# Attention masks as TensorE products, paired weight pieces, an earlier first expert tile and eight row buffers in an attention and mixture-of-experts kernel

## The chip, the cores and the metric

One core of one Trainium2 chip runs the kernel. The metric is the device time of one execution in microseconds (us). The core has TensorE (PE, matrix products and transposes), VectorE (DVE), ScalarE (ACT), GpSimd (POOL), the SyncE queue (SP), which here only issues transfers, and 16 DMA engines.

## What is computed

Sixteen batches of 100 queries attend to 1,444 keys of width 128. A mixture of eight experts (top two) follows over all 1,600 tokens. Cut to what matters:

```python
def xattn(input, memory, mask, w_input, dot_scale):   # input (16,100,128), memory (16,1444,128)
    att = (input @ w_input.T) + (input * dot_scale) @ memory.T - 1e+30 * mask[:, None, :]
    return softmax(att) @ memory

def moe(x, W_router, W_gate, W_up, W_down):           # 8 experts, F = 512
    gates, indices = top_k(softmax(x @ W_router.T), 2); gates = gates / gates.sum(-1)
    for e in experts:
        out += weight_e * ((silu(x @ W_gate[e].T) * (x @ W_up[e].T)) @ W_down[e].T)
    return out

x = x + tanh(g_xattn) * xattn(layernorm(x), ctx_1024, mask, ...)
x = x + tanh(g_ffn) * moe(layernorm(x), ...)
```

## The kernel before

Every engine has its own program, written out by hand in order; semaphores connect them. There is no scheduler, so what stands ahead of an instruction in its engine's program is what it queues behind.

**Attention, 16 steps.** Step b on TensorE is: the scores of batch b (L970, three products of 512, 512 and 420 columns, in float32 two passes each), the transposes of the softmax weights of batch b-1 (L980, 12), the transposes of the keys of batch b+1 (L957, 12), then the products of the softmax weights of b-1 with the keys (L990, 12, two passes), with the transpose of the second layer norm's result of batch b-2 (L998), its router product (L1004) and, every other step, the ranks (L1015, L1017) between them. ACT moves two thirds of the transposed keys out of PSUM and applies the score's scale and bias (L583), moves the transposed weights (L593) and computes the exponential (L627). DVE moves the last third (L702), adds the mask and takes the row maximum in one instruction (L741), and does residual, statistics, top two and ranks. POOL does the layer norms, the gates and scatters of the token rows into a DRAM table `slots`, sorted by expert (L508).

**Transfers of the attention.** All are issued by SP in program order: keys (720 KB a batch), a mask row broadcast to 100 partitions (564 KB a batch), and a 256 KB piece of the gate and up weights in each step. The masks of batches 0 and 1 come raw and ACT scales them (`scale_mask`); for the others DVE scales all 16 rows once (L869), ACT stores them to DRAM (L645) and SP broadcasts from there. ACT rounds each weight piece (L604, `round_weights`) after the exponential of a step, and DVE takes the rounding's rest (L729, `split_weights`). The 2 MB of down weights go out in four parts in steps 10 to 13, between the others (L338).

**Expert tiles.** There are 32 tiles of 128 token rows. The first eight (`EARLY`) are taken from what the first ten batches are known to fill, so that they can start before routing ends. In tile step k TensorE transposes the rows of tile k+1 (L1061), does gate and up of tile k (L1071 to L1073, six products of 512 columns), transposes the hidden values of tile k-1 (L1082) and multiplies tile k-2 by the down weights (L1093). ACT rounds the transposed rows (L653), applies silu (L662) and empties the hidden and result banks (L668, L674); DVE takes the rest of the rounding (L878) and multiplies gate, up and routing weight (L901). POOL scatters the results (L556). SP loads the rows into four buffers (L385), each load after the hidden values of four tiles before. Ahead of tile 8's load SP waits for `late_ready`, for the scatters of the last batches, and for eight clears of table tails (`clear_tail`, L388 reads a row number into a register, L389 issues the transfer); these stand behind the load of row block 6 and ahead of that of block 7.

**End.** When all results are stored, SP loads the first result of each token in four parts and ACT the second one (L408, L684), DVE adds both to x (L914, L917), and SP stores each part when its second addition is done (L411).

## Time and profile before

| | us |
|---|---|
| three runs, median | 287.19 |
| lowest and highest | 286.39, 293.68 |
| the profiled execution, its own time | 289.13 |
| its span in the trace | 287.3 |

Mean granted TensorE clock over the span: 0.941. By the page's own sums TensorE is busy 84% of the span (and its weight loads 69%), DVE 48%, ACT 47%, POOL 44%. Such shares are means over stages with different limits, so the reading below goes stage by stage.

### The profile page before, as it was taken

What the parts mean: (1) busy time and instruction counts of PE and PEld (TensorE: products, weight loads), DVE (VectorE), ACT (ScalarE), POOL (GpSimd) and SP (SyncE); (2) the same over time, 40 slices, a digit from 0 to 9 for tenths busy, and PEclk for the clock granted to TensorE, in tenths of its full rate; (3) what the DMA queues carried; (4) which work ended last, traced back from release to release, by engine and by line L of the source; (5) the groups of instructions that cost most, each with busy time, mean ns of one, the idle gap of its engine ahead of it and who ended that gap; (6) DMA issues with size and microseconds to landing.
All of it is one profiled execution on the core that took longest, in us unless ns stands there. A gap on an engine that the chain in (4) does not pass through costs nothing.

```text
span 287.3 us, 5727 instructions
## 1 busy us (share of the span) xinstructions
PE 241.9 (84%) x1602; PEld 199.2 (69%) x1603; DVE 137.4 (48%) x437; ACT 136.1 (47%) x295; POOL 126.0 (44%) x227
## 2 busy tenths in 40 slices
PE   7888498999999999999698896099999999999300
PEld 6657387777778887777578685089888878888200
DVE  1246238766666666675575553314343333433033
ACT  1466257555556665554546542226454554545100
POOL 4070403334754678877836877203323323233300
PEclk9999989999999999999899999669999999999855
DMA  5968877887788789999711022211111111110055
GB/s 135 219 191 202 191 191 205 204 195 205 196 201 204 199 207 220 224 230 244 241 44 50 5 65 75 65 28 49 38 56 40 55 37 37 55 37 30 27 182 161
DMA packets 19175, 37.65 MB, mean 131 GB/s; under 512 B 3722, under 2 KB 11090, under 8 KB 19150
## 3 DMA queue, kind: packets, MB, share of 16 engines
q1 hardware_dynamic: 15398, 32.65, 45.6%
q0 software_dynamic: 2560, 3.77, 4.5%
q10 hardware_dynamic: 1192, 0.92, 1.1%
q8 instruction: 13, 0.21, 0.3%
q14 instruction: 12, 0.10, 0.1%
HBM read 32.05 MB, written 5.27 MB: 130 GB/s over the span
## 4 chain that ended last, share of the span: by engine, by line
PE 60%; DMA 20%; SPq 5%; issue 5%; ACT 3%; DVE 2%; POOL 2%; another core or an unknown queue 1%; POOLq 0%; DVEq 0%; ACTq 0%
PE psum L990 12%; DMA ctx_sb<-in_ctx 11%; PE psum L1093 8%; PE psum L970 8%; PE psum L1071 6%; PE psum L957 6%; PE psum L1073 5%; DMA x_all<-in_x 5%; PE psum L1072 5%; PE psum L1082 5%; DMA ctx_sb<-results 3%; PE psum L980 2%; SPq L388 2%; PE psum L1061 1%; ACT probsT L593 1%
## 5 line engine op out<-in xcount | busy, mean ns | idle before, releaser
L556 POOL DMA_INDIRECT results<-y_sb,dest x32 | 30.8, 963 | 64.2 <-DVE dest L890 51.9
L990 PE MATMUL psum<-ctx_sb,probsT 120*100 120x128 f32 (+1 forms) x384 | 48.5, 278 | 1.0 <-issue 1.0
L901 DVE SCALAR_TENSOR_TENSOR scores<-probs,row_in,psum 128x512 f32<-128x512 f32 x32 | 23.9, 747 | 47.3 <-ACT probs L662 45.4
L990 PEld LDWEIGHTS psum<-ctx_sb,probsT 120*100 120x100 f32 (+1 forms) x384 | 44.4, 171 | 1.2 <-issue 1.2
L970 PE MATMUL psum<-ctxT,qT 128*100 128x512 f32 (+1 forms) x96 | 42.6, 581 | 0.2 <-issue 0.2
L662 ACT ACTIVATE probs<-psum 128x512 f32<-128x512 f32 x32 | 19.1, 597 | 43.4 <-PE psum L1073 36.2
L508 POOL DMA_INDIRECT slots<-pair_rows,slot_i x32 | 33.0, 1032 | 8.8 <-issue 8.8
L957 PE MATMUL psum<-identity,ctx_sb 120*128 120x120 f32 (+1 forms) x192 | 26.0, 291 | 11.7 <-DMA ctx_sb<-in_ctx 4.7
L1093 PE MATMUL psum<-w_down,hidT 128*128 x256 | 34.9, 280 | 0.8 <-ACT y_sb L674 0.6
L1093 PEld LDWEIGHTS psum<-w_down,hidT 128*128 128x128 f32 x256 | 32.0, 196 | 1.2 <-issue 1.2
L957 PEld LDWEIGHTS psum<-identity,ctx_sb 120*128 120x128 f32 (+1 forms) x192 | 22.3, 154 | 14.8 <-DMA ctx_sb<-in_ctx 7.7
L1071 PE MATMUL psum<-w_hi,rowT_hi 128*128 x64 | 28.8, 449 | 2.1 <-issue 1.7
L741 DVE CUSTOM_DVE_ANT_0 scores<-psum,maskb 100x1444 f32<-100x1444 f32 x16 | 26.5, 1659 | 7.6 <-PE psum L970 7.6
L437 POOL TENSOR_SCALAR var<-mv 100x1 f32<-100x1 f32 x16 | 4.8, 299 | 54.3 <-DVE mv L724 53.9
L970 PEld LDWEIGHTS psum<-ctxT,qT 128*100 128x100 f32 x96 | 15.4, 171 | 18.0 <-issue 18.0
L1073 PE MATMUL psum<-w_hi,rowT_lo 128*128 x64 | 25.7, 402 | 0.0
L583 ACT ACTIVATE ctxT<-psum,wi_col,ds_col 128x484 f32<-128x484 f32 (+1 forms) x32 | 22.6, 749 | 6.5 <-PE psum L957 3.8
L1072 PE MATMUL psum<-w_lo,rowT_hi 128*128 x64 | 25.5, 398 | 0.0
L627 ACT ACTIVATE probs<-scores,negmax 100x1444 f32<-100x1444 f32 x16 | 24.0, 1497 | 0.0
L588 ACT ACTIVATE qT<-psum 128x100 f32<-128x100 f32 x16 | 4.0, 250 | 39.8 <-PE psum L980 37.0
L593 ACT ACTIVATE probsT<-psum 120x400 f32<-120x400 f32 (+1 forms) x48 | 20.8, 510 | 3.6 <-PE psum L980 3.6
L702 DVE TENSOR_SCALAR ctxT<-psum,ds_col,wi_col 128x480 f32<-128x480 f32 x16 | 12.4, 776 | 19.4 <-PE psum L957 19.4
(126 smaller groups left out, 377.3 us busy)
## 6 DMA issues: line engine op xcount, KB each, us to landing
ctx_sb<-in_ctx SPq DMA_DIRECT2D x16, 720.0 KB
maskb<-mask_scaled SPq DMA_DIRECT2D x14, 564.1 KB
w_raw<-in_w_experts SPq DMA_DIRECT2D x16, 256.0 KB, 9.7
row_in<-slots SPq DMA_DIRECT2D x32, 65.0 KB
w_down<-in_w_experts SPq DMA_DIRECT2D x4, 512.0 KB
maskb<-in_mask SPq DMA_DIRECT2D x2, 564.1 KB
ctx_sb<-results SPq DMA_DIRECT2D x4, 200.0 KB
ctx_sb<-results ACTq DMA_DIRECT2D x4, 200.0 KB
```

Of the source, the lines that this page charges most:

```text
L508: nc.gpsimd.indirect_dma_start(slots, bass.IndirectOffsetOnAxis(ap=slot_i[:, b, j:j + 1], axis=0), pair_rows[:, b, j, :], None).then_inc(s ...
L556: nc.gpsimd.indirect_dma_start(results, bass.IndirectOffsetOnAxis(ap=dest[:, s:s + 1], axis=0), y_sb[:, s, :], None).then_inc(y_stored[s], 16)
L627: nc.scalar.activation(probs[0:Q, :], scores[0:Q, :], ACT.Exp, bias=negmax[:, b % 2:b % 2 + 1], accum_out=rowsum[:, b % RING:b % RING + 1] ...
L741: nc.vector.tensor_tensor_reduce(out=scores[0:Q, :], in0=scores_ps[0:Q, 0:K], in1=maskb[:, b % 2, :], scale=1.0, scalar=LOWEST, op0=ALU.ad ...
L901: nc.vector.scalar_tensor_tensor(out=hidden[k % 2], in0=silu[k % 2], scalar=row_in[:, s, D:D + 1], in1=up_ps[k % 2], op0=ALU.mult, op1=ALU ...
L957: last = nc.tensor.transpose(ring_ps[g][:, at:at + rows[c]], ctx_sb[0:rows[c], s, c, :], identity[0:rows[c], 0:rows[c]])
L970: last = nc.tensor.matmul(scores_ps[0:Q, n:n + m], qT[:, b % 2, :], ctxT[:, n:n + m], start=True, stop=True)
L990: last = nc.tensor.matmul(attn_ps[0:Q, 0:D], probsT[0:rows[c], c, :], ctx_sb[0:rows[c], b % RING, c, :], start=(c == 0), stop=(c == CHUNKS ...
L1071: nc.tensor.matmul(ps, rowT_hi[:, o, :], hi, start=True, stop=False)
L1072: nc.tensor.matmul(ps, rowT_hi[:, o, :], lo, start=False, stop=False)
L1073: last = nc.tensor.matmul(ps, rowT_lo[:, o, :], hi, start=False, stop=True)
L1093: last = nc.tensor.matmul(y_ps, hidT[:, o, c * P:(c + 1) * P], w_down[:, bass.ds(e * F + c * P, P)], start=(c == 0), stop=(c == FC - 1))
```

## The change

1. The masks of batches 0 and 1 are no longer loaded as broadcasts. The 16 raw mask rows go out second on SP's queue; `select` is a matrix whose row b is one for batch b; a product `select[:, b]` with the scaled mask rows starts the accumulation in the scores' bank and the score products add to it. DVE's addition gets a zero row for these two. The store of the scaled rows moves ahead of ACT's evictions. TensorE's three warming products behind the first transposes are gone.
2. Weight pieces follow a table `ROUNDED`: none before step 2, two in steps 6, 8 and 10, the last in step 14. The down weights go out all behind the loop. x comes in four parts.
3. Tile 0: its rows are transposed into a bank of the scores, and its gate and up products stand ahead of the last batch's attention products.
4. There are eight row buffers; SP issues all eight early row blocks and then five tail clears; ACT issues the other three, one after each of its tile steps 4, 5 and 6. The tables of the late tiles come one tile step earlier on DVE.
5. At the end SP loads parts 0 and 2 of both results, ACT parts 1 and 3; the output is laid out by query, so that each query's four batches are one run in DRAM (the host puts it back in place).

The core of the diff:

```diff
+MASKED = 2
+ROUNDED = {2: (0,), 3: (1,), 4: (2,), 5: (3,), 6: (4, 5), 7: (6,), 8: (7, 8), 9: (9,), 10: (10, 11), 11: (12,),
+           12: (13,), 13: (14,), 14: (15,)}
+SP_TAILS = 5
...
-        row_in = sb("row_in", [P, RING, ROW])
+        row_in = sb("row_in", [P, YRING, ROW])
...
             load_x(0)
+            sp.dma_start(mask_rows, mask).then_inc(mask_raw, 16)
             load_ctx(0)
-            load_raw_mask(0)
             load_x(1)
-            sp.dma_start(mask_rows, mask).then_inc(mask_raw, 16)
             load_ctx(1)
-            load_raw_mask(1)
             load_x(2)
             load_ctx(2)
-
-            for b in range(B - 2):
+            sp.wait_ge(mask_stored, 16)
+            load_mask(MASKED)
+            load_ctx(RING - 1)
+            load_x(3)
+
+            for b in range(1, B - 2):
                 sp.wait_ge(scores_done, b + 1)
-                if b == 0:
-                    sp.wait_ge(mask_stored, 16)
                 load_mask(b + 2)
-                if b == 0:
-                    load_ctx(RING - 1)
-                load_weights(b)
-                if 1 <= b and b + RING - 1 < B:
+                for c in ROUNDED.get(b + 1, ()):
+                    load_weights(c)
+                if b + RING - 1 < B:
                     sp.wait_ge(attn_raw, b)
                     load_ctx(b + RING - 1)
...
-                if b >= 10:
-                    load_down(b - 10)
-            load_weights(B - 2)
-            load_weights(B - 1)
+            for m in range(4):
+                load_down(m)
...
-                wait(sp, hidden_done, n - RING + 1)
+                wait(sp, hidden_done, n - YRING + 1)
...
-                if n == EARLY - 2:
+                if n == EARLY - 1:
                     sp.wait_ge(tails_ready, 1)
-                    for e in range(E):
+                    for e in range(SP_TAILS):
                         clear_tail(e)
...
-            for m in range(CUTS):
+            for m in range(0, CUTS, 2):
                 sp.dma_start(first_sb[:, m * CUT:(m + 1) * CUT, :], pairs(0, m)).then_inc(first_loaded[m], 16)
+            for m in range(0, CUTS, 2):
+                sp.dma_start(second_sb[:, m * CUT:(m + 1) * CUT, :], pairs(1, m)).then_inc(second_loaded[m], 16)
             for m in range(CUTS):
                 sp.wait_ge(second_added, m + 1)
-                sp.dma_start(out[m * CUT:(m + 1) * CUT, :, :].rearrange("b q d -> q b d"),
-                             x_all[:, m * CUT:(m + 1) * CUT, :]).then_inc(out_stored, 16)
+                sp.dma_start(out[:, m * CUT:(m + 1) * CUT, :], x_all[:, m * CUT:(m + 1) * CUT, :]).then_inc(out_stored, 16)
...
-                    if b == 0:
-                        scale_mask(1)
-                    if b >= 1:
-                        round_weights(b - 1)
-                    if b == B - 1:
-                        round_weights(B - 1)
+                    for c in ROUNDED.get(b, ()):
+                        round_weights(c)
...
             copy_qT(0)
+            act.wait_ge(mask_scaled_done, 1)
+            act.dma_start(mask_scaled, mask_rows).then_inc(mask_stored, 16)
             evict_ctxT(0, 0)
             evict_ctxT(0, 1)
-            scale_mask(0)
...
+            def between(n):
+                e = SP_TAILS + n - 4
+                if 0 <= n - 4 and e < E:
+                    if e == SP_TAILS:
+                        act.wait_ge(tails_ready, 1)
+                    clear_tail(e)
+
+            rowT_high(0, 0, first_rowT_ps)
             nc.scalar.activation(warm[:, :], wi_col[:, :], ACT.Silu)
-            copy_xn2T(B - 2)
-            over_tiles(act, tile_step)
+            for g in range(GROUPS):
+                copy_probsT(B - 1, g)
+            over_tiles(act, tile_step, between)
...
+            nc.vector.memset(maskb[:, 1, :], 0.0)
+            dve.wait_ge(identity_done, 1)
+            nc.vector.tensor_copy(select[:, :, :], identity[0:B, 0:MASKED].unsqueeze(2).to_broadcast([B, MASKED, Q])).then_inc(select_done, 1)
             statistics1(0)
             statistics1(1)
+            dve.wait_ge(mask_raw, 16)
+            nc.vector.tensor_scalar(mask_rows, mask_rows, NEG, None, ALU.mult).then_inc(mask_scaled_done, 1)
...
+            def add_mask(b):
+                pe.wait_ge(select_done, 1)
+                pe.wait_ge(mask_scaled_done, 1)
+                wait(pe, scores_done, b)
+                for n in range(0, K, 512):
+                    m = min(512, K - n)
+                    nc.tensor.matmul(scores_ps[0:Q, n:n + m], select[:, b, :], mask_rows[:, n:n + m], start=True, stop=False)
+
             def score(b):
+                if b < MASKED:
+                    add_mask(b)
...
             transpose_ctx(0)
-            keep_warm(3)
...
+            pe.wait_ge(scores_done, B)
+            transpose_rows(0, 0, first_rowT_ps)
             transpose_probs(B - 1, False)
+            pe.wait_ge(early_ready, 1)
+            pe.wait_ge(w_lo_done, B)
+            gate_up(0, 0)
             ranks(LAST - 1)
             attend(B - 1, 0, 2)
-            pe.wait_ge(early_ready, 1)
             pe.wait_ge(probsT_done, B * GROUPS)
-            transpose_rows(0, 0)
+            transpose_rows(0, 1)
             attend(B - 1, 2, GROUPS)
-            transpose_xn2(B - 2)
-            pe.wait_ge(w_lo_done, B)
-            pe.wait_ge(down_loaded, 16 * 4)
```

On TensorE, from the transposes of the first keys (into `psum` from `ctx_sb`) to the second scores (from `ctxT` and `qT`), the program stood so before:

```order
L957 MATMUL psum<-identity,ctx_sb 128x120 x8
L935 MATMUL psum<-identity 128x128 x3
L970 MATMUL psum<-ctxT,qT 100x512 x2
L970 MATMUL psum<-ctxT,qT 100x420
L939 MATMUL psum<-identity,xn 128x100
L957 MATMUL psum<-identity,ctx_sb 128x121 x4
L957 MATMUL psum<-identity,ctx_sb 128x120 x8
L935 MATMUL psum<-identity 128x128 x4
L970 MATMUL psum<-ctxT,qT 100x512 x2
```

And it stands so now, with the mask rows in the first columns of `w_down`:

```order
L973 MATMUL psum<-identity,ctx_sb 128x120 x8
L983 MATMUL psum<-w_down,select 100x512 x2
L983 MATMUL psum<-w_down,select 100x420
L996 MATMUL psum<-ctxT,qT 100x512 x2
L996 MATMUL psum<-ctxT,qT 100x420
L955 MATMUL psum<-identity,xn 128x100
L973 MATMUL psum<-identity,ctx_sb 128x121 x4
L973 MATMUL psum<-identity,ctx_sb 128x120 x8
L951 MATMUL psum<-identity 128x128 x4
L983 MATMUL psum<-w_down,select 100x512 x2
L983 MATMUL psum<-w_down,select 100x420
L996 MATMUL psum<-ctxT,qT 100x512 x2
```

A mask product of the same shape as the score's now stands ahead of each of the first two scores, and the three warming products (L935) are gone.

On TensorE at the hand-over to the tiles, from the transposes of the last softmax weights to tile 0's gate and up (reads of `row_in` are row transposes, of `pair_rows` the layer norm's), before:

```order
L980 MATMUL psum<-identity,probs 120x100 x8
L1015 MATMUL psum<-chosen,before 100x24
L1017 MATMUL psum<-passed,ones 100x24
L990 MATMUL psum<-ctx_sb,probsT 100x128 x8
L1061 MATMUL psum<-identity,row_in 128x128
L990 MATMUL psum<-ctx_sb,probsT 100x128 x4
L998 MATMUL psum<-identity,pair_rows 128x100
L1061 MATMUL psum<-identity,row_in 128x128
L1066 TENSOR_LOAD tile_expert
L1066 ISA x2
L1071 ISA
L1071 MATMUL psum<-w_hi,rowT_hi 128x512
```

and now (the first products of gate and up, and what is behind the six):

```order
L1087 MATMUL psum<-identity,row_in 128x128
L1007 MATMUL psum<-identity,probs 121x100 x4
L1007 MATMUL psum<-identity,probs 120x100 x8
L1092 TENSOR_LOAD tile_expert
...
L1099 MATMUL psum<-w_hi,rowT_lo 128x512
L1042 MATMUL psum<-chosen,before 100x24
L1044 MATMUL psum<-passed,ones 100x24
L1017 MATMUL psum<-ctx_sb,probsT 100x128 x8
L1087 MATMUL psum<-identity,row_in 128x128
L1017 MATMUL psum<-ctx_sb,probsT 100x128 x4
L1025 MATMUL psum<-identity,pair_rows 128x100
L1087 MATMUL psum<-identity,row_in 128x128
```

Tile 0's row transpose and its six products moved from behind the last attention products (L990, now L1017) to ahead of them; tile 1's row transpose took the place between them.

ACT's queue had no tail clears before. Now, behind the result copy (L674) of its tile step 4, and in the same way of steps 5 and 6:

```order
L646 ACTIVATE rowT_hi<-psum 128x128
L659 ACTIVATE probs<-psum 128x512
L666 ACTIVATE hidT<-psum 128x512
L674 ACTIVATE y_sb<-psum 128x128
L649 TENSOR_LOAD tail_row
L649 ISA x2
L650 ISA
L650 DMA slots<-empty 128x130
```

Three of SP's eight clears went to ACT, each tied to the end of one of its tile steps.

## Rows read from the trace of the kernel before

**Rows 1.** The page: DMA share in tenths, GB/s, in 40 slices of 7.2 us.
```profile
DMA  5968877887788789999711022211111111110055
GB/s 135 219 191 202 191 191 205 204 195 205 196 201 204 199 207 220 224 230 244 241 44 50 5 65 75 65 28 49 38 56 40 55 37 37 55 37 30 27 182 161
```
**Rows 2.** Windows: stretch, length, busy of PE, PEld, DVE, ACT, POOL, clock, DMA share, GB/s.
```profile
50.24:125.06 74.82, 73.44 (x543) 58.43 (x542) 49.03 (x163) 44.34 (x89) 44.55 (x78) 1.00 0.86 207
177.11:185.89 8.78, 0.00 (x0) 0.00 (x1) 2.68 (x8) 1.25 (x3) 3.88 (x4) 0.77 0.24 69
185.89:192.03 6.14, 5.73 (x19) 4.76 (x20) 1.11 (x3) 1.47 (x3) 0.00 (x0) 0.50 0.09 22
192.03:269.23 77.20, 75.93 (x496) 65.75 (x494) 27.31 (x74) 39.38 (x102) 25.52 (x27) 1.00 0.15 42
```
**Rows 3.** Timeline of the start: start, length, engine, line, what, idle before.
```profile
8.42 2.64 PE L957 MATMUL psum<-identity,ctx_sb 121*128 121x121 f32 x12 [1.67 <-ACT qT L588]
...
12.14 3.79 PE L970 MATMUL psum<-ctxT,qT 128*100 128x512 f32 x6
...
16.75 1.46 PE L957 MATMUL psum<-identity,ctx_sb 121*128 121x121 f32 x12 [0.73 <-DMA ctx_sb<-in_ctx]
...
19.27 2.64 PE L970 MATMUL psum<-ctxT,qT 128*100 128x512 f32 x6 [0.17 <-issue]
```
**Rows 4.** Timeline of the start, steps 1 to 3.
```profile
27.79 2.59 PE L970 MATMUL psum<-ctxT,qT 128*100 128x512 f32 x6
...
34.13 0.63 ACT L604 ACTIVATE w_hi<-w_raw 128x512 fp32r<-128x512 f32 x1 [6.71 <-DMA w_raw<-in_w_experts]
...
35.45 2.64 PE L957 MATMUL psum<-identity,ctx_sb 121*128 121x121 f32 x12 [3.87 <-ACT probsT L593]
```
**Rows 5.** The chain that ended last: start, length, what. Scores of steps 4 and 6.
```profile
50.24 2.42 PE psum L970 x6
...
66.82 2.42 PE psum L970 x6
```
**Rows 6.** Timeline of TensorE at steps 13 to 15.
```profile
125.06 2.59 PE L970 MATMUL psum<-ctxT,qT 128*100 128x512 f32 x6
...
133.58 2.59 PE L970 MATMUL psum<-ctxT,qT 128*100 128x512 f32 x6
...
140.15 2.09 PE L957 MATMUL psum<-identity,ctx_sb 121*128 121x121 f32 x12 [2.79 <-DMA ctx_sb<-in_ctx]
...
146.30 2.59 PE L970 MATMUL psum<-ctxT,qT 128*100 128x512 f32 x6
```
**Rows 7.** Timeline of the hand-over: tile 0's products on TensorE, ranks, SP's tail clears.
```profile
160.20 0.49 PE L1071 MATMUL psum<-w_hi,rowT_hi 128*128 x1 [0.68 <-issue]
...
168.99 0.28 PE L1015 MATMUL psum<-chosen,before 100*100 100x24 f32 x2
...
170.84 12.49 SPq L389 DMA_DIRECT2D slots<-empty  x8
```
**Rows 8.** Timeline of TensorE, the head of tile step 6.
```profile
185.89 0.47 PE L1061 MATMUL psum<-identity,row_in 128*128 128x128 f32 x1 [8.78 <-DMA row_in<-slots]
```
**Rows 9.** The chain: an SP register step, a clear, row block 7; timeline: block 8.
```profile
180.46 0.70 SPq L388
...
183.01 0.33 SPq L389
...
184.10 1.74 DMA row_in<-slots
...
186.17 0.36 SPq L385 DMA_DIRECT2D row_in<-slots  x1
```
**Rows 10.** Timeline of the end: first, second and last additions.
```profile
277.08 0.69 DVE L914 TENSOR_TENSOR x_all<-x_all,ctx_sb 100x512 f32<-100x512 f32 x1 [11.63 <-DMA ctx_sb<-results]
277.88 0.69 DVE L917 TENSOR_TENSOR x_all<-x_all,ctx_sb 100x512 f32<-100x512 f32 x1
...
282.05 0.69 DVE L914 TENSOR_TENSOR x_all<-x_all,ctx_sb 100x512 f32<-100x512 f32 x1 [0.17 <-DMA ctx_sb<-results]
283.22 0.69 DVE L917 TENSOR_TENSOR x_all<-x_all,ctx_sb 100x512 f32<-100x512 f32 x1 [0.47 <-DVE x_all L914]
```

135 lines of the change are left out of this document (71 added, 64 removed).

## The prediction, made before the changed kernel ran

> **What bounds the kernel now.** I read the chain of work that ended last, then the timeline stretch by stretch, then windows of the same stretches. Five stages came out.
>
> *Start, 0 to 50.24.* The first scores run from 12.14, the second from 19.27, the third from 27.79, the fifth from 50.24 [rows 3, 4, 5]. An undisturbed pair of steps takes 66.82 - 50.24 = 16.58 us [rows 5], but the third to fifth took 22.45. ACT had waited 6.71 us for the first weight piece, with the softmax weights of batch 1 queued behind, and TensorE 3.87 us for ACT [rows 4].
>
> *Attention, 50.24 to 125.06.* TensorE is busy 73.44 of 74.82 us, at a DMA share of 0.86 and 207 GB/s [rows 2]. TensorE is the bound and transfers are near theirs.
>
> *Its end.* Steps 13 and 14 took 146.30 - 125.06 = 21.24 us, with a 2.79 us wait for the last keys [rows 6]. In these slices the DMA digits stand at 9 and the rate at 230 to 244 GB/s, the highest of the trace [rows 1]: the down weights share the queue with these keys.
>
> *Tiles.* Tile 0's products begin at 160.20 [rows 7]. Step 5 ends at 177.11, then TensorE does nothing for 8.78 us [rows 2, 8]: block 7 stands behind eight clears on SP, 170.84 to 183.33 [rows 7]. The next step runs at clock 0.50 and takes 6.14 us; after it 27 steps take 77.20 us, 2.86 each [rows 2].
>
> *End.* DVE's last addition ends at 283.9, the span at 287.3 [rows 10].
>
> **The change, part by part.** *Masks.* Added are two groups of six passes of the scores' shape: 2.59 us each at full clock [rows 4]. The first group begins right behind the key transposes, at 8.42 + 2.64 = 11.1 [rows 3], where warming products stood. The first scores took 3.79 us, which is about three passes at half clock and three at full [rows 3], so the clock rose near 14.6; from 11.1 the group takes 4.3 us, to 15.4, and the scores end at 18.0. It can begin there only if DVE has scaled the 16 rows. DVE's zero row and `select` come before; nothing in the trace shows a fill of 1,444 columns, I bound it between nothing and the 1.66 us of DVE's mask instruction of that width and take that it is hidden: DVE is idle until x lands. The keys of batch 1 came at 16.75 [rows 3]; 1.13 MB of raw masks less in the queue, at some 200 GB/s [rows 1], bring them before 18. Transposes and warming take 19.27 - 16.75 = 2.5, to 20.5; the second group 2.6, so the second scores start at 23.1, 3.8 us later than before. To the third 8.52 less 0.8 for the keys' lateness, 30.9. From there two undisturbed steps: the weight piece is asked for later and rounded a step later, behind less traffic. 30.9 + 16.6 = 47.5 against 50.24: **2.7 us gained**. The bounds are no gain (the 5.9 us of losses half stay) and 5.9 (the products lie wholly in waits).
>
> *Weights in twos.* The same 16 roundings (0.63 us each [rows 4]) on ACT and 16 on DVE; in the undisturbed stretch ACT is busy 44 and DVE 49 of 75 us [rows 2], so a second piece in a step is hidden; uncovered it would be three times 0.63, 2 us. The 2 MB of down weights go behind the keys; the mask of a step, one piece and the keys then make 1.5 MB in 8.3 us, what the undisturbed stretch carries. Steps 13 and 14 should take 16.6 instead of 21.24: **4.7 us gained** (bounds 2.8, the wait alone, and 5). The down weights are wanted only in tile step 2. What is late next is the first row block, behind 2 MB or 9 us of them on the same queue, and that is needed some 18 us after they are issued.
>
> *First tile.* Before, tile 0's products began 13.9 us after the last scores (160.20 - 146.30), behind the attention products, after a gap of 0.68 us [rows 7]. Now they stand in the gaps ahead of those and tile 1's begin about where tile 0's did: the rows for both are there, ACT's copies of the softmax weights stand behind its table load but ahead of their use. So the tiles run one step ahead, and step 6 ends where step 5 did, 30.8 us after the last scores. The last residual, and so the last ranks (168.99, 22.7 us after the last scores) and SP's first clear (170.84, 24.5 us [rows 7]), keep their place within 1 us or come some 1 us sooner.
>
> *Buffers and clears.* Block 7 no longer waits, block 8 does: for all eight clears. SP's five begin near 24 us after the last scores and take 5.5 us at 1.09 each, or 7.8 at the mean of 12.49 / 8 [rows 7, 9], done by 32. But ACT's last one stands behind its tile step 6, so it cannot be issued before 30.8 + 0.4 for the copy + 0.75 for the register. From a clear's issue to block 8's was 186.17 - 183.01 = 3.16 us, and a block lands in 1.74 [rows 9]. TensorE stops at the head of step 7 for 0.4 + 0.75 + 3.16 + 1.74 = 6.05 us. It resumes at 36.9 with step 7; before it resumed at 39.6 with step 6. Both then pay one slow step. Gain 2.7 + 2.86 = **5.6 us**. Bounds: 0 if ACT's clears go as slowly as SP's slowest, and 12 if no stop is left.
>
> *End.* Parts landed about 1.66 us apart, both results of a part together (277.08 to 282.05 for four [rows 10]). Now the first results of parts 0 and 1 come first, then of 2 and 3, and the second result of part 0 only third, near 280.4. Seven additions at 0.8 [rows 10] follow: 286.0 against 283.9. The last store, 3.4 us before, finds an empty queue; from the 2.1 us of a clear (3.16 less 1.09) and 200 KB at 240 GB/s [rows 1] I take 2.9. **1.5 us lost** (bounds: none, and 2.1 with the old store). The Trainium skill, "DMA: Bandwidth & Descriptors", section Specifications, names 512 B as the smallest transfer at line rate; the old output runs are just 512 B, so by that rule the new layout brings nothing and the loss would be 2.1; no row here separates the two.
>
> **Sum.** 2.7 + 4.7 + 5.6 - 1.5 = 11.5 us. The span of 287.3 becomes 275.8, the profiled execution's 289.13 becomes 277.6. The median of the runs is 287.19, 1.9 below that execution; I take the sum off the median: **275.7 us**.
>
> **Rivals.**
> 1. *ACT's clears are slow* (281). SP's register steps took 0.70 us each from 174 to 182 [rows 9], and a clear has four that matter, so about 2.9 us. ACT is busy some 1.75 of 2.86 us per tile (39.38 over 27 steps is 1.46 [rows 2], and register work and waits for its own copies some 0.3 more by my estimate), so a clear of 2.9 holds each of two tiles up by 1.8 and the last comes 1.8 later: 5.4 us. Against it: SP's first clears took 1.1.
> 2. *The start gives nothing* (278.5). The product groups cost their 5.2 us and more at half clock, and the weight piece is late again. For it: the queue was full in this stretch [rows 1]. Against it: 1.13 MB less.
> 3. *The stop shrinks* (270). If ACT issues its last clear earlier relative to TensorE than I put it, or the start gains its upper bound. Little speaks for it: the order on ACT is fixed.
> 4. *Pairs of weight pieces fill the queue; slower than before* (289). In steps 5, 7 and 9 SP now asks for mask, two pieces and keys, 1.84 MB in 8.3 us or 222 GB/s, against the 230 to 244 at which keys came late [rows 1]. If each pair costs the 4.3 us that step 14 lost, 12.9, plus 0.3 in the steps between, the 11.5 gained are gone: 289. It decides where the queue saturates below 222 GB/s. Against it: the step between carries one piece, and keys are asked for 12 us ahead. The Trainium skill, "DMA: Bandwidth & Descriptors", section "Why a DMA increments its semaphore by 16 and not by 1", says that 100 partitions use only ten of the engines, so that the masks load these ten more; by it a pair step puts 140 KB on the busiest engine, against 156 KB in the steps that came late, 90%, and the time would be this rival's if that were enough to saturate. The trace doesn't tell engines apart.
>
> That the change does not do what it says is part of 1 and 2: TensorE stands still 8.8 us at the tiles with or without it.
>
> **How the numbers follow.** My forecast, 272 to 280: 0.56. Rival 1: 0.16. Rival 2: 0.12. Rival 3: 0.09. Rival 4: 0.07. The range of 8 in 10 takes in all of rival 1 and 2 and the upper part of 3: 270.5 to 282. A measurement of this kernel tells 2% from no change, 5.7 us: faster below 281.4. The forecast, rivals 2 and 3 and nearly half of rival 1 (0.07) lie there: 0.84. Within 2%: 0.12, the rest of rival 1 and half of rival 4. Slower: 0.04, the tail of rival 4.
>
> **What would show it.** Start: the fifth scores near 47.5, no wait of ACT for a weight piece above 1 us, the second mask group right behind the warming products. Attention: no wait for keys above 0.5 us in steps 5 to 10 (else rival 4) and none at step 14. Hand-over: tile 1's products 13 to 14 us after the last scores. Tiles: one stop near 6 us at block 8, ended by its load, with ACT's third clear the last issued; if it is above 9 us, rival 1. End: DVE's third addition late, the last near 286 less what was gained. I am wrong if TensorE waits anywhere ahead of tile 0 for rows or for the rounded weights.

## The result: slower, not faster

Four runs of the changed kernel have a median of 291.86 us (289.44 to 293.69), four of the kernel before 286.79 (285.70 to 293.68); the ratio is 1.018, 95% interval 1.011 to 1.026. The forecast was 275.7. On another chip, where the kernel before took 281.84, the changed one took 282.78: ratio 1.006 (1.002 to 1.010). So it is slower by 0.6 to 1.8%, and the expected 11.5 us are missing. Some executions of a kernel fall into a slower state; medians are over all executions, ratios leave the slow ones out.

The page of the changed kernel, whose profiled execution took 291.94 us (span 290.1): busy tenths of TensorE, clock, DMA share and rate in 40 slices of 7.25 us, to be held against [rows 1].

```profile
PE   6999999999999999999979895489999999998100
PEclk9999999999999999999997999759999999999855
DMA  5973577778778887886621022121112111000163
GB/s 129 222 191 85 136 194 200 193 196 225 210 211 198 220 223 205 214 225 204 252 73 31 21 57 65 37 58 47 56 38 57 36 46 46 18 29 25 53 211 96
```

Windows of the changed kernel (columns as in [rows 2]): the undisturbed stretch, steps 13 and 14, the hand-over, tile step 6, the stop, the step behind it, the rest.

```profile
50.68:125.89 75.21, 73.77 (x544) 58.60 (x543) 50.96 (x165) 46.37 (x93) 44.31 (x78) 1.00 0.81 210
125.89:142.73 16.84, 16.48 (x122) 12.93 (x121) 12.61 (x46) 9.95 (x20) 13.16 (x22) 1.00 0.77 256
142.73:154.69 11.96, 10.14 (x71) 8.02 (x69) 6.26 (x26) 5.86 (x13) 8.81 (x16) 0.97 0.26 65
176.62:184.46 7.84, 4.60 (x18) 3.54 (x18) 1.85 (x4) 2.66 (x6) 3.28 (x4) 0.80 0.13 41
184.46:189.46 5.00, 0.01 (x1) 0.00 (x0) 0.00 (x0) 0.28 (x1) 0.96 (x1) 0.84 0.14 40
189.46:195.30 5.84, 5.47 (x20) 4.50 (x21) 1.11 (x3) 1.47 (x3) 0.00 (x0) 0.53 0.24 60
195.30:269.40 74.10, 72.90 (x477) 63.15 (x475) 26.23 (x71) 37.88 (x98) 24.53 (x26) 1.00 0.13 39
```

The last scores start at 142.73 instead of 146.30. From there to the last down product's start it is 125.6 us, against 121.8 before, and from the first load of the results to the span's end 17.20, against 14.67. That is -3.6 + 3.8 + 2.5 = +2.7, the difference of the two spans within 0.1; the 4.6 us between the last down product's start and the first load are the same in both. In what follows S is the start of the last scores, and a place is told by its distance from S.

*Start.* TensorE of the changed kernel: start, length, line, tiles with the rows and columns of one product (16x512: contracted over 16 rows).

```profile
10.93 5.13 PE L983 MATMUL psum<-w_down,select 16*100 16x512 f32 x6
15.99 5.08 PE L996 MATMUL psum<-ctxT,qT 128*100 128x512 f32 x6
...
23.80 2.66 PE L983 MATMUL psum<-w_down,select 16*100 16x512 f32 x6
26.39 2.67 PE L996 MATMUL psum<-ctxT,qT 128*100 128x512 f32 x6
34.28 2.59 PE L996 MATMUL psum<-ctxT,qT 128*100 128x512 f32 x6
```

The first two groups run wholly at half speed, 10.2 us for twelve passes. From 26.39 on the steps take 7.9 and 8.2 us, without the waits of [rows 4]. The fifth scores start at 50.68. Before, the timeline has them at 50.08 (the 50.24 of [rows 5] is from the chain, which counts from the end of the product before), so the start is 0.6 us longer.

*Hand-over and step 6.* The changed kernel: tile 0's row transpose and who takes it up (number in brackets: idle before), then the last gate and up product of tile 5, ACT's silu of it, and TensorE's next transposes of hidden values.

```profile
149.35 0.28 PE L1087 MATMUL psum<-identity,row_in 128*128 128x128 f32 x1
151.82 0.28 ACT L646 ACTIVATE rowT_hi<-psum 128x128 fp32r<-128x128 f32 x1 [2.47 <-remote]
152.58 0.49 PE L1097 MATMUL psum<-w_hi,rowT_hi 128*128 x1 [1.82 <-issue]
...
174.18 0.39 PE L1099 MATMUL psum<-w_hi,rowT_lo 128*128 x1
179.30 0.60 ACT L659 ACTIVATE probs<-psum 128x512 f32<-128x512 f32 x1 [4.03 <-PE psum L1099]
181.52 1.08 PE L1108 MATMUL psum<-identity,scores 128*128 128x128 f32 x4 [3.24 <-ACT hidT L666]
```

TensorE's product is done at 149.63, and ACT, which has nothing else to do, takes it at 151.82. Tile 5's is done at 174.57, and ACT takes it at 179.30. The trace's semaphore events say the same: TensorE's increment for the first comes at 151.80, for the second at 179.28. These late increments were there in the kernel before as well:

```profile
175.39 0.39 PE L1073 MATMUL psum<-w_hi,rowT_lo 128*128 x1
...
181.90 0.60 ACT L662 ACTIVATE probs<-psum 128x512 f32<-128x512 f32 x1 [6.16 <-remote]
```

The products were done at 175.78, and ACT's silu of them began at 181.90. There TensorE stood in its stop for block 7 anyway [rows 8].

*Stop.* SP's and ACT's tail clears, block 8's load and TensorE's stop, changed kernel.

```profile
169.31 7.10 SPq L390 DMA_DIRECT2D slots<-empty  x5
...
174.56 0.39 ACTq L650 DMA_DIRECT2D slots<-empty  x1
...
181.55 0.35 ACTq L650 DMA_DIRECT2D slots<-empty  x1
...
185.17 0.34 ACTq L650 DMA_DIRECT2D slots<-empty  x1
187.55 3.71 SPq L386 DMA_DIRECT2D row_in<-slots  x4
189.46 0.48 PE L1087 MATMUL psum<-identity,row_in 128*128 128x128 f32 x1 [5.00 <-DMA row_in<-slots]
```

*End.* First three additions and the stores, changed kernel. The second one waits 2.53 us for the second result of part 0.

```profile
277.31 0.69 DVE L928 TENSOR_TENSOR x_all<-x_all,ctx_sb 100x512 f32<-100x512 f32 x1 [11.59 <-DMA ctx_sb<-results]
280.53 0.69 DVE L931 TENSOR_TENSOR x_all<-x_all,ctx_sb 100x512 f32<-100x512 f32 x1 [2.53 <-DMA ctx_sb<-results]
281.14 0.68 DVE L928 TENSOR_TENSOR x_all<-x_all,ctx_sb 100x512 f32<-100x512 f32 x1
281.25 4.48 SPq L414 DMA_DIRECT2D out<-x_all  x4
```

### The profile page after: what moved, and what is told of

Read it like the earlier page. It is cut to its first block, busy times and chain, and to the rows that moved or that the text cites. A ratio compares the mean times of both kernels' runs of the same rounds, so it can differ in the third digit from the quotient of the medians.

```text
span 290.1 us, 5742 instructions
## 1 busy us (share of the span) xinstructions
PE 249.8 (86%) x1608; PEld 199.9 (69%) x1609; DVE 138.4 (48%) x439; ACT 133.2 (46%) x293; POOL 126.0 (43%) x227
## 4 chain that ended last, share of the span: by engine, by line
PE 80%; DMA 5%; ACT 4%; issue 4%; DVE 2%; POOL 1%; another core or an unknown queue 0%; SPq 0%; POOLq 0%; ACTq 0%; DVEq 0%
PE psum L1017 15%; PE psum L996 14%; PE psum L1119 10%; PE psum L973 8%; PE psum L1097 7%; PE psum L1099 6%; PE psum L1098 5%; PE psum L1108 5%; PE psum L1007 3%; PE psum L983 3%; DMA ctx_sb<-results 2%; ACT probsT L595 2%; ACT qT L590 1%; PE psum L1087 1%; DMA x_all<-in_x 1%
## 5 line engine op out<-in xcount | busy, mean ns | idle before, releaser
L1017 PE MATMUL psum<-ctx_sb,probsT 120*100 120x128 f32 (+1 forms) x384 | 49.0, 280 | 0.0
L1017 PEld LDWEIGHTS psum<-ctx_sb,probsT 120*100 120x100 f32 (+1 forms) x384 | 44.7, 172 | 0.2 <-issue 0.2
L996 PE MATMUL psum<-ctxT,qT 128*100 128x512 f32 (+1 forms) x96 | 44.0, 596 | 0.0
L1119 PE MATMUL psum<-w_down,hidT 128*128 x256 | 35.5, 284 | 0.8 <-ACT y_sb L674 0.6
L1119 PEld LDWEIGHTS psum<-w_down,hidT 128*128 128x128 f32 x256 | 32.5, 199 | 1.4 <-issue 1.4
L973 PE MATMUL psum<-identity,ctx_sb 120*128 120x120 f32 (+1 forms) x192 | 24.1, 277 | 2.8 <-ACT qT L590 0.4
L973 PEld LDWEIGHTS psum<-identity,ctx_sb 120*128 120x128 f32 (+1 forms) x192 | 20.8, 147 | 6.0 <-issue 5.4
L1108 PE MATMUL psum<-identity,scores 128*128 128x128 f32 x128 | 20.3, 283 | 3.4 <-ACT hidT L666 3.2
```

The costliest lines, as they stand in the source:

```text
L973: last = nc.tensor.transpose(ring_ps[g][:, at:at + rows[c]], ctx_sb[0:rows[c], s, c, :], identity[0:rows[c], 0:rows[c]])
L996: last = nc.tensor.matmul(scores_ps[0:Q, n:n + m], qT[:, b % 2, :], ctxT[:, n:n + m], start=(b >= MASKED), stop=True)
L1017: last = nc.tensor.matmul(attn_ps[0:Q, 0:D], probsT[0:rows[c], c, :], ctx_sb[0:rows[c], b % RING, c, :], start=(c == 0), stop=(c == CHUNKS ...
L1108: last = nc.tensor.transpose(hidT_ps[:, c * P:(c + 1) * P], hidden[k % 2][:, c * P:(c + 1) * P], identity[:, :])
L1119: last = nc.tensor.matmul(y_ps, hidT[:, o, c * P:(c + 1) * P], w_down[:, bass.ds(e * F + c * P, P)], start=(c == 0), stop=(c == FC - 1))
```

## Experiments

Four sets of four kernels, each set on a chip of its own with the kernel before beside it; only ratios compare across sets, and distances within a trace. Single runs of a kernel scatter by 2 to 4 us, so phases tell more than medians.

### The start: rows of a product and the clock

**The score products first, the mask product behind them.** `a_score_first`, its edit in short:

```diff
-    if b < MASKED: add_mask(b)                      # start=True, stop=False
     matmul(scores_ps[0:Q, n:n + m], qT, ctxT, start=True, stop=(b >= MASKED))
+    if b < MASKED: last = add_mask(b)               # start=False, stop=True
```

> The changed kernel, with the mask products of batches 0 and 1 behind the score products instead of ahead of them. Theory: products over 16 rows of the array do not bring TensorE out of half speed (in the trace of the changed kernel all six passes of the first mask group took 0.86 us each, and so did the six of the first score, to 21.0 us; before, the speed rose at about 14.6). Then here the first scores run as before (about 3.8 us from about 11.9), the mask group behind them at full speed (2.6 us), and the second scores' group starts about 3 us earlier: 2.5 to 3.5 us less than the changed kernel. Rival: the speed rose late because the keep-warm products are missing; then the mask group behind the scores changes nothing, within 1 us.

291.41 us, ratio 1.015 (1.007 to 1.023); fifth scores at 51.64. TensorE of this kernel:

```profile
11.01 5.09 PE L994 MATMUL psum<-ctxT,qT 128*100 128x512 f32 x6 [1.03 <-DVE ctxT L712]
16.03 2.66 PE L982 MATMUL psum<-w_down,select 16*100 16x512 f32 x6
...
19.32 2.61 PE L973 MATMUL psum<-identity,ctx_sb 121*128 121x121 f32 x12 [0.39 <-issue]
```

Nothing won, and the theory's forecast for the first scores failed: they took 5.09 us and not 3.8, though they contract over 128 rows and nothing of the mask stands ahead of them. So this run alone doesn't decide between rows and moment. It gives a hint: the key transposes behind the first mask group run at half speed (2.61 us instead of 1.43), and so do those behind the second one, at 29.80 (2.64 us), with 1.27 us of other transposes at full speed between.

**The same mask product over 112 rows.** `c_mask_112` puts the mask rows at partitions 96 to 111 and zeros above, so that a product contracts over 112 rows instead of 16:

```diff
+            nc.vector.memset(w_down[0:FROM, 0:K], 0.0)
...
-                    nc.tensor.matmul(scores_ps[0:Q, n:n + m], select[:, b, :], mask_rows[:, n:n + m], start=True, stop=False)
+                    nc.tensor.matmul(scores_ps[0:Q, n:n + m], select[:, b, :], w_down[0:FROM + B, n:n + m], start=True, stop=False)
```

> The changed kernel, but the mask product contracts over 112 rows (96 rows of zeros above the 16 mask rows) where the changed kernel has 16; the product's count, columns and place are the same. Theory A (in the changed kernel the clock stayed low through 5.13 us of mask products and 5.08 us of the first scores because the products over 16 rows do not count as work for it): with 112 rows the clock rises inside or right behind the first mask group, the first scores take under 4 us instead of 5.08, they end near 18 instead of 21.0, and the fifth scores start near 48 instead of 50.68. Rival B (the number of rows does not matter; what counts is the time since the last idle stretch, or the data): mask group and first scores take 5.1 and 5.1 us again and the fifth scores start at 50.5 to 51.5. The time follows: about 2.7 us below the changed kernel under A, none under B.

287.55 us, ratio 0.996 (0.992 to 1.001). TensorE:

```profile
10.79 2.90 PE L985 MATMUL psum<-w_down,select 112*100 112x512 f32 x6
13.53 2.59 PE L998 MATMUL psum<-ctxT,qT 128*100 128x512 f32 x6
...
21.18 2.59 PE L998 MATMUL psum<-ctxT,qT 128*100 128x512 f32 x6
29.00 2.59 PE L998 MATMUL psum<-ctxT,qT 128*100 128x512 f32 x6
```

Same place, same count, same columns, and both groups run at full speed but for the first 0.6 us: 5.3 instead of 10.2 us. The fifth scores start at 45.40, 5.3 us earlier than in the changed kernel and 2.1 earlier than forecast. One trace could owe this to the moment at which the clock happened to rise, so here are all traces with mask products ahead of the scores:

| rows of the mask product | traces | first mask group, us | first scores, us | fifth scores start |
|---|---|---|---|---|
| 16 | 8 | 4.65 to 5.13 | 4.02 to 5.14 | 49.54 to 51.47 |
| 112 | 5 | 2.90 to 4.28 | 2.59 in each | 45.40 to 46.90 |

The two sets don't overlap, and each of the last three chips ran both kinds, so neither the moment nor the chip explains it, and theory A holds: in no trace did TensorE go from 1.2 to 2.4 GHz during a group over 16 rows, and in all five it did during the first group over 112 rows. That 16 rows also fail to keep the higher clock is seen less often: it fell within or soon behind a mask group in `a_score_first` (twice), `a_old_handover` (second scores 4.36 us) and `a_tails_sp` (4.23 us), and stayed in the second mask groups of the six others. What happens between 16 and 112 rows, or with the 16 rows at another place in the array, was not run.

The time follows only in part. `c_mask_112` starts its last scores at 140.30, 2.4 us earlier than the changed kernel and not 5.3: TensorE waits for keys at 82.95 (0.60 us) and 92.56 (1.24 us), and the steps around them are longer. In `d_joined` below, with the same mask products, there is no such wait.

**The old masks with everything else changed.** `c_old_masks` (raw broadcasts, `scale_mask` and three warming products back).

> The changed kernel with the masks of batches 0 and 1 as before it (raw broadcasts, scaled by ACT, three warming products), and everything else as changed: weight table, down weights behind the loop, first tile, buffers, end. Theory A (the table of weight pieces alone removed the waits of steps 1 to 3, and the mask products cost more than they save): first scores at 12.1, second at 19.3 to 21, third near 28, and then undisturbed steps of 8.2 us, the fifth scores near 44.5 (bounds 43.5 and 46.5), 4 to 7 us earlier than in the changed kernel, and the time that much lower. Rival B (the raw masks in the queue were what made steps 2 and 3 late): the keys or masks come late again and the fifth scores start at 49 or later.

289.88 us, ratio 1.003 (0.998 to 1.008). The third and fourth scores start at 28.30 and 36.53 as forecast, but the fifth at 49.05: TensorE waits for the keys of batch 4 until 43.22. Both theories are half right. Without the mask products the waits of steps 1 and 2 [rows 4] are gone, so the weight table suffices for those; with the 1.13 MB of raw masks back in the queue keys are late one step further on. The change's idea of the mask as a product was sound, and its 16 rows spoiled it.

### The stop: who clears

**All eight clears on SP.** `a_tails_sp`:

```diff
-SP_TAILS = 5
+SP_TAILS = 8
```

> The changed kernel, with all eight tail clears on SP. Theory A: the stop at row block 8 hangs on ACT's third clear (issued at 185.2 us, block 8 at 187.6); with all on SP the clears end near 181 and the stop shortens by 3 to 5 us. Theory B: the clears are slowed by something else at that time (SP's register steps took 0.7 us each until 178.4, and ACT stood 4 us until 179.3), so three more clears on SP take until about 184 and the time stays within 1.5 us.

287.90 us, ratio 1.004 (0.998 to 1.009), and relative to S: block 8's load issued at 37.9 instead of 44.8, tile 7's products at 40.65 instead of 47.58, and at tile 8's row transpose TensorE waits 0.38 us instead of 5.00 (a wait of 2.34 us for a late increment stays in step 6). From S to the last products it is 119.1 us instead of 125.6. Theory A holds: ACT's third clear, tied to the end of its tile step 6, was the bound.

**The old hand-over.** `a_old_handover` puts tile 0's row transpose and products back behind the attention products.

> The changed kernel, with the order of the hand-over on TensorE, ACT and DVE put back (tile 0's products behind the last attention products). Theory: moving tile 0's products ahead removed no work; it made TensorE wait 1.8 us for tile 0's rows and run the attention products behind them at half speed, so tile step 2 begins 20.2 us after the last scores instead of 18.2. Then this kernel is 1.5 to 3 us faster than the changed one. Rival (that of the forecast): the early products fill gaps and put the tiles ahead, so that putting them back costs 1 to 3 us.

290.06 us, ratio 1.011 (1.004 to 1.018). From S, tile 0's products start at 15.1 instead of 9.9, but tile 1's at 17.3 instead of 16.9 and tile 6's at 33.2 instead of 33.9; then the stop, and tile 8's at 52.3 instead of 52.6. The last products start at 125.6 in both. The new hand-over has lost its lead by tile 6; neither the gain of the theory nor the loss of the rival is there.

### The late increments

**Pauses between scatters.** In all ten traces of the first pair and the first two sets some of TensorE's increments come 1 to 6 us late, always in the stretches in which POOL issues indirect scatters back to back. No increment of ACT, DVE or POOL does. `c_spaced` is the kernel with all clears on SP and this:

```diff
             def scatter(b):
                 for j in range(2):
+                    if b >= 12:
+                        pause()      # three small power instructions, 1.7 us
```

and the same ahead of the second and third result scatters (`SP_TAILS` and the body of `pause` left out here).

> The changed kernel with all eight tail clears on SP, and on POOL three small power instructions (about 1.7 us together) ahead of each of the last eight token scatters and of the second and third result scatters, so that no two scatters stand back to back. The run with the clears on SP alone showed, during the four scatters in a row, ACT and DVE idle 2.9 and 1.6 us although their inputs were there, both until the fourth was through, and 2.7 and 2.2 us on ACT in the next series, with SP's register steps at 0.7 us. Theory A (a series of GpSimd's indirect DMA instructions holds up the semaphores or instruction supply of the other engines): with pauses no such idle stretch above 1.3 us is left on ACT and DVE, tile 0's products start 1.5 to 2.5 us earlier relative to the last scores (8 to 8.7 instead of 10.2), and SP's eight clears take under 9.5 us instead of 11.7 from first to last. Rival B (the stretches come from the engines' own programs, as from code loading): they stay where they are in the program, with 2 to 3 us each. The late scatters themselves end some 8 to 12 us later, so row block 8 may come later by up to 6 us under either; the time alone tells nothing.

297.06 us, ratio 1.031. The four scatters of batches 10 and 11, which this edit does not touch, still stand back to back until 151.02:

```profile
148.27 0.28 PE L1099 MATMUL psum<-identity,row_in 128*128 128x128 f32 x1
150.03 0.99 POOL L520 DMA_INDIRECT slots<-pair_rows,slot_i  x1 [0.30 <-issue]
151.79 0.28 ACT L658 ACTIVATE rowT_hi<-psum 128x128 fp32r<-128x128 f32 x1 [3.51 <-remote]
```

Their delay is there. Behind 152, where the pauses are, no increment is late by more than 0.6 us, SP's clears take 7.7 us from first to last instead of 11.7, and ACT's wait in step 6 is gone. The late scatters then hold block 8 back to S + 50.5, with a stop of 15.2 us; hence the time. On this chip A holds as far as this run can tell: the pauses also moved the scatters to later, and it does not part the two.

**Pauses elsewhere, and the kernels without them, on other chips.** `d_space_early` pauses only ahead of the scatters of batches 10 and 11; `d_before_spaced` is the kernel before with pauses.

> The changed kernel with two small power instructions on POOL (about 1.2 us) ahead of each of the four token scatters of batches 10 and 11, and nothing else. In the changed kernel these four stand back to back from 146.86 to 151.86, and the increments that TensorE owes for the attention products of batch 14 and for tile 0's row transpose (done near 149.6) come only at 151.8. In the run with pauses between the later scatters (163 to 195) no increment after 152 was late by more than 0.6 us, while these four, left back to back, kept their 3.2 us. Theory A (scatters back to back delay TensorE's increments, whatever else runs): here the delay at tile 0 falls below 0.8 us, tile 0's products start 1.5 to 2.3 us earlier relative to the last scores (7.6 to 8.4 instead of 9.85), while the delays near 167, 174 and 180, of the series that stay as they are, remain. Rival B (the delay at tile 0 has to do with the row loads on SP or with code that is new there): tile 0's products start at 9.5 or later. Rival C (what helped was that the scatters came later, not the pauses): the same as A for the sign but the delay moves to the next increments within the series. The median: 0 to 2 us below the changed kernel's.

> The kernel before with the same pauses on POOL and nothing else. There four scatters stand back to back from 150.07, four from 163.42 and seven from 171.93, TensorE's increments came up to 6.1 us late at 181.9, and SP's register steps took 0.70 us each, so that eight clears took 12.2 us from the first's issue (24.5 us after the last scores) to the last's (36.7). Theory A: no increment is late by more than 0.8 us, the clears' last is issued at 31 to 34 us after the last scores instead of 36.7, row block 7 at 33 to 35 instead of 37.8, TensorE's stop at step 6 shrinks from 8.8 to 4 to 6.5 us, but the stop then meets block 8, which waits for the later scatters, for up to 3 us: 0 to 3 us faster. Rival B (pauses only delay): clears as slow as before and the time the same or up to 4 us slower.

285.72 and 289.33 us, ratios 1.017 (1.008 to 1.027) and 1.017 (1.002 to 1.032, from two executions). The theory could not be tested here: no increment was late in any trace of this chip, with pauses or without. Tile 0's products did start at S + 7.95, but they do so in `e_after` too, which has no pause. What the pauses did here is make TensorE wait 2.3 us for POOL's last layer norm. So "scatters back to back delay TensorE's increments" is not true everywhere. It held in the first pair and on the chips of the first two sets, and not on the chips of the last two, and on these the kernel before itself is 5 to 7 us faster. What differs between these chips stays open. One more difference is on record: the ten traces with late increments hold 3539 to 3682 records of semaphore increments, the eight without 4142 to 4179, though the programs are nearly the same and no instruction is missing. Between S - 30 and S + 30, where most of the scatters stand, it is 645 in the changed kernel's first trace and 1116 in its second, `e_after`. In the same stretches SP's register steps, 0.02 to 0.27 us each in `e_before`, end up to 0.70 us apart. So the records of increments are lost where increments are late, and that the recording itself has a part in the delay is a rival that no run here excludes.

**Both kernels on such a chip.** `e_before` and `e_after`, unchanged.

> The kernel before, unchanged, for a trace on the same chip as the other three. If late increments (theory A: they are a matter of the chip, and cost each kernel some us) are absent on this chip: SP's clears 1.1 us apart, the last issued at 33 to 34 us after the last scores instead of 36.7, block 7 at 34 to 35, time 280 to 283. If they are present: as in the first trace, 36.7, 37.8 and 287.

> The changed kernel, unchanged. On a chip without late increments, theory A (the order of the clears is what costs): ACT's third clear is issued near 37 us after the last scores, block 8's load near 39.6, tile 8's step starts near 46.9 and the time is 0.5 to 2% above that of the kernel before. Rival B (the late increments cost the changed kernel what it gained, since it no longer hides them behind a stop): without them it is faster than the kernel before by 1% or more. On a chip with them: 42.4, 44.8 and 52.6 us, and 1 to 2% slower.

281.43 and 282.78 us. `e_after` at the same two places:

```profile
149.34 0.27 PE L1087 MATMUL psum<-identity,row_in 128*128 128x128 f32 x1
149.65 0.28 ACT L646 ACTIVATE rowT_hi<-psum 128x128 fp32r<-128x128 f32 x1 [0.31 <-PE psum L1087]
150.67 0.50 PE L1097 MATMUL psum<-w_hi,rowT_hi 128*128 x1
...
165.46 4.73 SPq L390 DMA_DIRECT2D slots<-empty  x5
176.23 0.34 ACTq L650 DMA_DIRECT2D slots<-empty  x1
178.62 3.71 SPq L386 DMA_DIRECT2D row_in<-slots  x4
180.50 0.47 PE L1087 MATMUL psum<-identity,row_in 128*128 128x128 f32 x1 [4.97 <-DMA row_in<-slots]
```

ACT takes tile 0's rows 0.03 us after the product, and SP's five clears need 4.7 us instead of 7.1. The stop is still 4.97 us, since ACT's third clear is issued only at S + 33.5; SP's own fifth is out at S + 27.1, and in `e_before` SP alone has issued all eight by S + 30.7. And in `e_before` the eight clears take 8.15 us instead of [rows 7]'s 12.49, and the stop shrinks too:

```profile
166.39 8.15 SPq L389 DMA_DIRECT2D slots<-empty  x8
...
177.34 0.48 PE L1061 MATMUL psum<-identity,row_in 128*128 128x128 f32 x1 [4.55 <-DMA row_in<-slots]
```

Without late increments the kernel before resumes 5.8 us earlier from S, at 33.8, and the changed one 8.9, at 37.8. The changed one then has one tile step less before it (78.8 us to the last products against 81.5), which does not make up for the 3.9 us. B falls: the change loses without late increments as well, by 0.6%. With them it loses 1.8%. There ACT's third clear comes 8.9 us later from S than here, behind a wait of ACT of 4.03 us for a late increment of TensorE (179.30 above), while the kernel before hid its longest one under its stop. How much of the difference each late increment makes was not measured: `a_old_handover` has them at other places, and its last products start at the same S + 125.6.

### The end: order of loads and layout

`a_old_end` has the old order of the loads and the old output; `c_old_loads` has all clears on SP, the old order, and the new layout (the core of its edit; SP's loads of second results and ACT's part of the order are put back in the same way):

```diff
-            for m in range(0, CUTS, 2):
+            for m in range(CUTS):
                 sp.dma_start(first_sb[:, m * CUT:(m + 1) * CUT, :], pairs(0, m)).then_inc(first_loaded[m], 16)
```

> The changed kernel, with the end put back: first results on SP, second on ACT, output by batch with runs of 512 B. The end from the load issue (272.9) to the end of the span (290.1) took 17.2 us against 14.7 before. Theory: this comes from the order of the loads, so putting it back saves 2 to 3 us. Rival: the stores by query are themselves slower (the last took 4.4 us against 3.4), which this run alone cannot tell from it.

> The changed kernel with all eight tail clears on SP, and the end's loads in the old order (SP loads the four parts of the first result, ACT those of the second), but the output still laid out by query with 2 KB runs. From the first load's issue to the end of the span the kernel before took 14.67 us, the changed kernel and its variants 16.75 to 17.20, and the variant with both the old loads and the old layout 15.77. Theory A (the order of the loads is what costs, the layout saves nothing): 15.5 to 15.9 us here, DVE's third and later additions about 1.3 us earlier than with the new order. Rival B (the order costs nothing and the new layout's stores are slower): 16.7 to 17.2. Rival C (the new layout saves up to 1 us): 14.7 to 15.2. The time should be 0 to 2.4 us under that of the variant with the clears on SP alone.

290.73 us (ratio 1.012, 1.002 to 1.022) and 287.98 (0.991, 0.983 to 0.999). From the first load to the end: 15.77 and 14.89 us, against 17.20 in the changed kernel and 16.4 to 17.3 in the eight other traces with the new order. First additions of `c_old_loads`:

```profile
272.44 0.69 DVE L924 TENSOR_TENSOR x_all<-x_all,ctx_sb 100x512 f32<-100x512 f32 x1 [11.93 <-DMA ctx_sb<-results]
273.23 0.69 DVE L927 TENSOR_TENSOR x_all<-x_all,ctx_sb 100x512 f32<-100x512 f32 x1
273.84 0.69 DVE L924 TENSOR_TENSOR x_all<-x_all,ctx_sb 100x512 f32<-100x512 f32 x1
```

The order costs about 2 us. The layout's share can't be told from zero: five traces with it and the old order gave 14.8 to 15.1, four with the old layout and order 14.67, 14.69, 15.22 and 15.77.

### The corrections together

`d_joined` and, on another chip, the same kernel as `e_joined`: 112 rows, all clears on SP, old order of the loads. `d_joined_spaced` adds pauses, `e_joined_old_handover` the old hand-over.

> Three corrections of the changed kernel that single runs have tried, together: the mask product over 112 rows, all eight tail clears on SP, and the end's loads in the old order with the output by query. If the gains add up relative to the changed kernel: 5.3 us at the start (fifth scores at 45.4 instead of 50.7), 2 to 5 us at the stop (tile step 8 starts 47 to 50 us after the last scores... 46 in one run, 46.9 in another, instead of 52.6), 2.3 us at the end (14.9 instead of 17.2): a span of 277 to 281 us. Theory A (the gains add): that. Rival B (an earlier start only meets a later stop, since the clears wait for the last batch's routing and the stop at block 8 absorbs what is gained before): the start's gain survives, since routing moves with the last scores, but of the stop's not more than 2 us are seen: 281 to 284.

> The kernel of three corrections (mask product over 112 rows, all clears on SP, the end's loads in the old order), again, on another occasion. Its ratio to the kernel before was 0.970 on one chip. If the gain is the kernel's (A), it is 0.96 to 0.98 here whatever the chip; if it was the luck of that chip and moment (B), above 0.985. Fifth scores near 45.5, block 8 issued 33 to 38 us after the last scores, end 14.8 to 15.1 us after the first load's issue.

> The kernel of the three corrections together, and pauses on POOL: two power instructions (1.2 us) ahead of each scatter of batches 10 and 11, one (0.6 us) ahead of each of the later token scatters and of the second and third result scatters. Theory A (scatters back to back delay TensorE's increments and SP's register steps): no delay above 0.8 us is left, tile 0's products start 7.6 to 8.4 us after the last scores, the wait of TensorE in tile step 6 (2.3 to 3.9 us in all variants) is gone, SP's clears take under 9.5 us from first to last instead of 10 to 12, and row block 8 is issued at 36 to 42 us after the last scores, then bound by the last scatters, which end some 5 us later. In sum 0 to 3 us faster than the same kernel without pauses. Rival B (0.6 us is too short a pause, or the later end of the scatters costs what the pauses give): the delays stay near 180, or block 8 comes later than 42; same time or up to 3 us slower.

> The same with the old hand-over: tile 0's products behind the last attention products again. In the changed kernel tile 0's products come 4 us earlier but tile 1's 3.6 us later than the step before did (16.93 against 13.90 + one step of 2.9 us is even), and TensorE waits for tile 0's rows ahead of the attention products. Theory A (moving tile 0's products neither removes nor adds work, and the stop at block 8 absorbs any difference): same time as the joined kernel within 1 us. Rival B (the earlier tile shortens the way to the last residual and routing, and with it the clears): 1 to 3 us slower than the joined kernel, the first clear 1 to 2 us later relative to the last scores.

| kernel | us | ratio | fifth scores | S | block 8's load, from S | last products, from S | end |
|---|---|---|---|---|---|---|---|
| e_before | 281.43 | 1.000 | 49.68 | 143.50 | 33.3 | 115.3 | 15.22 |
| e_after | 282.78 | 1.006 (1.002 to 1.010) | 50.78 | 142.72 | 35.9 | 116.6 | 16.91 |
| d_joined | 273.08 | 0.970 (0.960 to 0.980) | 45.59 | 137.70 | 33.3 | 114.7 | 15.02 |
| e_joined | 273.45 | 0.965 (0.954 to 0.977) | 46.87 | 138.98 | 33.5 | 113.5 | 15.01 |
| e_joined_old_handover | 272.75 | 0.971 (0.965 to 0.978) | 46.17 | 138.26 | 32.5 | 113.0 | 15.06 |
| d_joined_spaced | 281.45 | 1.004 (1.000 to 1.009) | 46.90 | 138.88 | 41.3 | 122.6 | 14.79 |

Joined, the corrections make the kernel 3 to 3.5% faster than the kernel before, with spans of 272.0 and 272.1. That is below the 277 to 281 of `d_joined`'s theory A, whose numbers came from traces with late increments; this chip showed none. The joined kernel was not run on a chip that shows them. The two traces of it differ by 1.3 us at the fifth scores and by 1.2 us from S to the last products, so much for what one trace can tell. The moved first tile brings nothing: with the old hand-over, on the same chip as `e_joined`, the last products start at S + 113.0 instead of S + 113.5, and the times are equal within their intervals. The pauses cost 8.4 us, all of the gain and more than the 3 us of rival B.

## Why the prediction was wrong, step by step

| step | forecast | first pair of traces | pair without late increments |
|---|---|---|---|
| start, to the fifth scores | -2.7 | +0.6 | +1.1 |
| steps 4 to 12, undisturbed | 0 | +0.2 | +0.2 |
| end of the attention | -4.7 | -4.4 | -2.1 |
| tiles, S to last products | -5.6 | +3.8 | +1.3 |
| end | +1.5 | +2.5 | +1.7 |
| sum | -11.5 | +2.7 | +2.2 |

**Start.** "From 11.1 the group takes 4.3 us" failed. It carried over the moment at which the clock rose before [rows 3] to products that contract over 16 rows instead of 128. They took 5.13, and the scores behind them another 5.08 instead of 2.6; the clock rose only at 20.9, not near 14.6. The rest of this term was right: no wait for a weight piece above 1 us, keys in time, the second group behind the warming products, undisturbed steps from the second scores on. With 112 rows the whole term came out: the fifth scores started at 45.40 to 46.90 in five traces, 0.6 to 2.1 us better than the forecast 47.5.

**End of the attention.** Right in mechanism and size: 16.84 us for two steps instead of the forecast 16.6, no wait for keys. Rival 4 (pairs of weight pieces fill the queue) is wrong for this kernel, the stretch 50.68 to 125.89 took 75.21 us against 74.98 from timeline to timeline; only `c_mask_112`, which gets there 5.3 us sooner, showed waits for keys in it, 1.8 us together.

**Tiles.** Three parts of this step failed.

1. "So the tiles run one step ahead, and step 6 ends where step 5 did." That counts work twice. Tile 0's six products moved from one side of the attention products to the other; both sides still have to be done. The sign that was to show the lead even came true, tile 1's products at S + 13.4 in `e_after` (S + 16.9 in the first trace). But in `e_before` tile 1's followed tile 0's by 1.7 us and not by a step of 2.86, at S + 14.4, and tile 5 starts at S + 26.34 in `e_after` and S + 26.31 in `e_before`. Nothing is a step ahead.
2. Rival 1 (ACT's clears are slow) was the nearest of the rivals, with another cause: the clears wait for ACT's tile steps, and these for TensorE's late increments. ACT's third clear was issued at S + 42.4, the forecast had S + 32. In `e_after`, without late increments, it was S + 33.5, and TensorE resumed at S + 37.8, 0.9 us from the forecast 36.9.
3. But there the kernel before resumes at S + 33.8, one step earlier in the program, instead of 39.6 [rows 8]. The sum compared an undisturbed changed kernel with a trace of the old one that had lost 6 us to late increments and to register steps of 0.70 us [rows 9]. These stood in the trace as an idle 6.16 us of ACT under TensorE's stop, where the prediction passed over them.

**End.** The mechanism is right: the second addition waits. But it waited 2.53 us, for a load that is issued fifth of eight, and with it seven additions of 0.70 each were still to come. The last store from issue to end took 4.7 us and not 2.9, so the hoped gain of the layout is missing: +2.5 instead of +1.5 (1.6 by the prediction's own terms, 2.1 less 0.5). The Trainium skill, "DMA: Bandwidth & Descriptors", section Specifications, by which 512 B runs are already at line rate and 2.1 us would be lost, was nearer.

**The chances.** 0.04 stood on slower, all of it on rival 4. None of the causes found was among the rivals, neither the clock under products of few rows, nor the double counting, nor the late increments.

## What to carry to other kernels

Ahead of a product that is put in to use an idle gap, ask at which of its two clocks TensorE stands there and whether the product's rows fill the array; padding 16 rows with zeros to 112 cost 1.26 us of an idle DVE and brought the fifth scores forward by 3.8 to 5.3 us in five traces. Moving work ahead of other work on the same engine moves nothing that both precede, so carry each tile's start through by hand. And a long idle stretch under a stop of another engine is a debt: before a change takes away that cover, find out what its engine waited for.

## What the runs showed of the hardware

- Products of 512 columns over 16 rows, back to back for 5.1 us, left TensorE at 1.2 GHz, and behind 2.66 us of them at 2.4 GHz the next transposes ran at 1.2 in `a_score_first`, though at 2.4 in the changed kernel; with the same products over 112 rows it rose and stayed, in five traces of five. The Trainium skill, "TensorE: Matmul & The Clock Gate", section "What's actually happening", has the clock follow how busy the engine has been, whatever is issued; these rows differ.
- The page's clock digits of the changed kernel stand at 9 in the slice from 7.25 to 14.5 us, where a pass takes 0.86 us instead of 0.43; in `e_after`, with the same 5.13 us for the first mask group, that slice reads 5. The first trace has no record of the clock before 20.9 us, and the page counts such a stretch as full speed; `e_after` has records, and they give 0.50 from 8.1 to 21.8 us. Where the two disagree, go by the lengths of the passes.
- TensorE's semaphore increments came up to 6.1 us after the end that the profile gives its products, in ten traces of eighteen. The Trainium skill, "Perfetto Trace Analysis", section "Tensor Engine Instruction (MATMUL, LD_WEIGHTS)", says that this end is an estimate, made before the write is acknowledged and the increment sent; so whether the products or only the increments are late can't be read from it. The rows of the consumer show it.
